# One of four normalisation tiles per attention head moved from GpSimd to VectorE, in a one-layer language-model tower on one core

## The reference, cut to what matters

```python
att = jnp.einsum('bhqd,bhkd->bhqk', q, k) / np.float32(np.sqrt(D))
att = att + jnp.exp(alibi_log_slopes)[None, :, None, None] * rel[None, None]
mask = pos[:, None] >= pos[None, :]
att = jnp.where(mask[None, None], att, -jnp.inf)
m = jnp.max(att, axis=-1, keepdims=True)
e = jnp.exp(att - m)
att = e / (1.0 + jnp.sum(e, axis=-1, keepdims=True))
out = jnp.einsum('bhqk,bhkd->bhqd', att, v)
```

## Time and profile before

| | us |
|---|---|
| median of 3 executions | 945.58 (944.63 to 945.79) |
| the profiled execution | 943.51 |
| its span | 941.7 |
| granted TensorE clock, mean of the span | 0.996 |

### The profile page before, as it was taken

The page is one execution under the profiler, slowest core; times in us unless marked ns, Lnnn a source line. Parts: engine busy times, 40 slices in busy tenths (PEclk is TensorE's granted clock), DMA queues, the critical chain, the costliest instruction groups (busy, mean ns, idle before and its releaser), DMA issues.

```text
span 941.7 us, 16997 instructions
## 1 busy us (share of the span) xinstructions
PE 872.0 (93%) x5660; PEld 680.4 (72%) x5660; DVE 581.7 (62%) x1779; ACT 728.0 (77%) x1622; POOL 627.7 (67%) x599
## 2 busy tenths in 40 slices
PE   7999978999999998999999999999899999999997
PEld 6888856777866786577766876777667866787585
DVE  5565636776684658475847575756756684658434
ACT  6855348998689869996889688877888689869843
POOL 6000069899686878688767878596868686868630
PEclk9999999999999999999999999999999999999999
DMA  9333360001000200020000100010001000000000
GB/s 262 73 112 112 125 190 1 1 1 56 2 1 1 79 1 2 1 73 7 2 1 24 56 1 1 23 58 1 1 23 57 1 1 1 23 2 1 1 23 23
DMA packets 23605, 33.56 MB, mean 36 GB/s; under 512 B 2608, under 2 KB 20176, under 8 KB 23520
## 3 DMA queue, kind: packets, MB, share of 16 engines
q1 hardware_dynamic: 19760, 19.01, 6.3%
q0 software_dynamic: 3760, 13.48, 5.0%
HBM read 17.80 MB, written 14.68 MB: 34 GB/s over the span
## 4 chain that ended last, share of the span: by engine, by line
PE 49%; ACT 13%; POOL 11%; issue 8%; DVE 6%; DMA 0%; POOLq 0%; DVEq 0%; ACTq 0%
PE ps L1388 12%; PE ps L1192 12%; POOL probs L783 9%; PE ps L1372 8%; PE ps L1360 5%; ACT probs L822 5%; PE ps L1361 4%; ACT turned_sb L829 4%; PE ps L1340 3%; DVE probs L994 2%; POOL token_rows L771 2%; PE ps L1200 1%; ACT k_hi L844 1%; ACT q_both L839 1%; PE ps L1334 1%
## 5 line engine op out<-in xcount | busy, mean ns | idle before, releaser
L783 POOL TENSOR_SCALAR probs<-probs,sums 128x512 f32<-128x512 f32 (+3 forms) x512 | 545.2, 1083 | 155.0 <-DVE sums L1001 154.6
L994 DVE CUSTOM_DVE_ANT_0 probs<-ps,causal,slope 128x512 f32<-128x512 f32 (+3 forms) x512 | 260.0, 547 | 162.0 <-PE ps L1361 161.5
L822 ACT ACTIVATE probs<-probs 128x513 f32<-128x513 f32 (+3 forms) x512 | 283.8, 556 | 34.9 <-DVE probs L994 27.4
L829 ACT ACTIVATE turned_sb<-ps 128x1280 f32<-128x1280 f32 x128 | 157.1, 1228 | 59.3 <-PE ps L1372 59.2
L1360 PE MATMUL ps<-k_hi,q_both 128*128 128x512 f32 (+3 forms) x512 | 181.0, 354 | 19.2 <-DVE probs L994 18.3
L1372 PE MATMUL ps<-ident,probs 128*128 128x128 f32 x1280 | 162.1, 274 | 5.3 <-POOL probs L783 5.3
L1388 PE MATMUL ps<-turned_sb,token_rows 128*64 128x512 f32 (+3 forms) x1024 | 152.0, 438 | 13.5 <-ACT turned_sb L829 13.5
L1361 PE MATMUL ps<-k_lo,q_both 128*128 128x512 f32 (+3 forms) x512 | 152.6, 324 | 0.0
L1372 PEld LDWEIGHTS ps<-ident,probs 128*128 128x128 f32 x1280 | 143.7, 142 | 6.8 <-POOL probs L783 6.5
L1388 PEld LDWEIGHTS ps<-turned_sb,token_rows 128*64 128x64 f32 x1024 | 75.2, 136 | 98.6 <-issue 82.6
L1360 PEld LDWEIGHTS ps<-k_hi,q_both 128*128 128x128 f32 x512 | 96.6, 189 | 61.1 <-DVE probs L994 34.9
(11 more groups left out here) (225 smaller groups left out, 1443.9 us busy)
## 6 DMA issues: line engine op xcount, KB each, us to landing
out_dram<-token_rows SPq DMA_DIRECT2D x7, 512.0 KB, 2.9
token_table<-made SPq DMA_DIRECT2D x4, 768.0 KB, 4.0
rows<-in_L_tok_codebook_dram SPq DMA_DIRECT2D x4, 512.0 KB, 9.9
w_f<-in_L_tok_W_dram SPq DMA_DIRECT2D x8, 256.0 KB, 6.1
early_rows<-made SPq DMA_DIRECT2D x4, 512.0 KB, 3.0
early_values<-xn SPq DMA_DIRECT2D x4, 512.0 KB, 3.0
token_table<-xn SPq DMA_DIRECT2D x4, 512.0 KB, 4.8
wo_f<-in_L_attn_Wo_dram POOLq DMA_DIRECT2D x1, 1024.0 KB, 10.3
```

Of the source, the lines that this page charges most:

```text
L783: ins = pool.tensor_scalar(at, at, recip[:, s % P_RING, q:q + 1], None, ALU.mult)
L822: act.activation(at, at, ACT.Exp, bias=least, scale=-1.0, accum_out=sums[:, s % P_RING, q:q + 1]).then_inc(exped, 1)
L829: act.activation(turned_sb[:, s % 2, :], turn_ps, ACT.Copy).then_inc(moved, 1)
L994: dve.tensor_tensor_reduce(out=probs[:, s % P_RING, start:end], in0=bank(unit % 2)[:, UNIT_AT[q]:UNIT_AT[q] + P * (q + 1)], in1=causal[:, ...
```

## The change

GpSimd no longer normalises row tile 0 of a head, the 128x128 block. VectorE does, in the next slot, behind the first minimum of the next head. TensorE's `turn` waits for both engines.

```diff
+    first_normed = sem("first_normed")
...
             def normalize(s):
                 pool.wait_ge(recip_done, s + 1)
-                for q in Q_ORDER:
+                for q in (3, 2, 1):
                     at = probs[:, s % P_RING, P_AT[q]:P_AT[q] + P * (q + 1)]
                     ins = pool.tensor_scalar(at, at, recip[:, s % P_RING, q:q + 1], None, ALU.mult)
                 ins.then_inc(normed, 1)
...
+            def normalize_first(s):
+
+                at = probs[:, s % P_RING, P_AT[0]:P_AT[0] + P]
+                dve.wait_ge(recip_done, s + 1)
+                dve.tensor_scalar(at, at, recip[:, s % P_RING, 0:1], None, ALU.mult).then_inc(first_normed, 1)
...
                 if s < ALL:
                     least_of(s, 0)
+                if 1 <= s <= ALL:
+                    normalize_first(s - 1)
+                if s < ALL:
                     least_of(s, 1)
                     least_of(s, 2)
...
             def turn(s):
                 pe.wait_ge(normed, s + 1)
+                pe.wait_ge(first_normed, s + 1)
```

## The result

The changed kernel takes **936.86 us** (median, 936.22 to 937.74) where the kernel before takes 945.68 on the same chip: ratio 0.9912, 95% interval 0.99 to 0.9925. It is 8.8 us faster. The forecast was 965.1 with 83% on slower, so the sign and the range are wrong. The profiled execution took 937.74 us, with a span of 935.9; TensorE's granted clock is 0.995 (0.996 before), so the clock plays no part.

The account below looks back on a forecast made before the run. TensorE was taken as the kernel's clock, GpSimd bounding only behind each gather. GpSimd's -5.3 us and VectorE's +3.1 and +21.7 made +19.5 us: 963.0 profiled, 965.1 as median; range from 947, its own upper end 984.

Parts of the forecast that it names:

- the two rows of 0.52 and 0.21 us: In the norm, VectorE's 128x4 tensor_scalar beside GpSimd's 128x128: both ended 0.03 us behind GpSimd's tile, read as a hold.
- The arrivals: VectorE reaches its new instruction at 187.69 and 412.97, inside GpSimd's 128x512; held 0.76 and 1.05 us to the tile's end.
- VectorE's terms: Cost of holds on VectorE's 128 new instructions reaching TensorE: +3.1 us in the first element, +21.7 in the seven later ones.
- 2.6 us per element in slots 7 to 12: Later elements: 1.5 us in slots 7 to 9 ahead of xn, 0.6 at slot 11 (y_lo), 0.5 at slot 12.
- The 0.5 us for slot 1: Later elements, slot 1 splitting K: the hold beyond VectorE's 0.56 us idle time delays k_lo and the turned copy, 0.5 us.
- The term for the opening slots: First element's two opening slots, where GpSimd still gathers: the new instruction costs 2 x 0.26 us.
- GpSimd's term: Behind the gathers, all six TensorE waits for GpSimd's normalisation go: -5.3 us, called the most this side can give.
- Rival 1: No hold worth the name, the tensor_scalar takes 0.26 us everywhere: -2.3 us, 943.3; chance 0.11.
- the new group's mean: Sign to check: VectorE's new x128 group averages near 1.0 us; 0.34 would be rival 1, 0.6 rival 2.
- Rival 2: Hold bounded at 0.35 us beyond the plain duration, instruction 0.6 us: +1.6 us, 947.2; chance 0.08.
- rival 3: GpSimd's next tile, 128x384, gets in first on some 60 uncovered slots: +75 us more, 1040; chance 0.04.
- Rival 4: VectorE's entries delay GpSimd's next tile, some 0.2 of 0.60 us per head returns: 1 us in all; no chance given.

Follow-up runs that it names:

- the probe: 105 trials behind the end of the kernel before: one GpSimd tensor_scalar of 512 to 128 columns against one delayed VectorE instruction; only the trace read, no kernel time.
- experiments 1, 4 and 6: 1: changed kernel without VectorE's normalisation of tile 0, ratio 0.9882; 4: changed kernel again, 0.9919; 6: VectorE's tile on heads 0, 1, 7, 8, 0.9887, and 1 again, 0.9879.
- experiment 2: Kernel before, GpSimd keeping all four tiles, plus an unused 128x128 tensor_scalar on VectorE at the same place: 945.74 us against 944.59, ratio 1.0005.
- the relief alone: Changed kernel with VectorE's new instruction and TensorE's wait left out, so row tile 0 is not normalised: 933.71 us, ratio 0.9882; repeated 933.51 us, 0.9879.
- the four-head version: Changed kernel with VectorE taking tile 0 only for heads 0, 1, 7 and 8 of each element: 934.45 us, ratio 0.9889; repeated 934.18 us, 0.9887.
- `early`: Changed kernel with VectorE's new instruction ahead of the first minimum, right behind the reciprocal that releases GpSimd: 938.25 us, ratio 0.9928.

## Why the prediction was wrong

**The step that failed is the reading of the earlier trace rows**: "VectorE's tensor_scalar is held until GpSimd's current instruction is over." The hold is no property of the whole tile. It comes in two stretches with a free one between, and the rows from which I read it were of 128 and 256 columns, where the probe has the instruction free at one or two of its starts 0.1 us apart, against four at 512 columns. Of the two rows of 0.52 and 0.21 us, the second was no hold: the probe's 128x4 lasts 0.22 us alone, so that it ended 0.03 us behind the tile was chance. xn's first 128x256, issued 0.52 us into a 128x256, was held by the second stretch, which I then carried over to the first half of a 128x512. The 0.52 us row itself is not reproduced: the probe's 128x4 issued 0.12 us into a lone 128x128 tile ends at 0.39, that of the trace at 0.62. That is 0.03 us behind the tile's end, where the probe's 128x4 ends from the second hold (0.02), so it looks as if it had missed the free stretch, as the one at 0.16 us above; GpSimd's tiles follow each other in both, and why they miss it stays open.

**The arrivals were right and decided the other way.** The earlier trace rows put VectorE at 0.80 and 0.51 us behind the start of GpSimd's 128x512. Both lie in the free stretch. In the changed kernel 28 of the new instructions start at about 0.5 us (0.45 to 0.55) and 22 at 0.8, with means of 288 and 283 ns. The timeline of both cases of the earlier trace rows after, and of one that meets a 128x384:

```profile
188.10 1.57 POOL L784 TENSOR_SCALAR probs<-probs,sums 128x512 f32<-128x512 f32 x1 [1.66 <-DVE sums L1002]
188.91 0.28 DVE L1008 TENSOR_SCALAR probs<-probs,sums 128x128 f32<-128x128 f32 x1
...
191.77 1.57 POOL L784 TENSOR_SCALAR probs<-probs,sums 128x512 f32<-128x512 f32 x1
192.18 0.36 DVE L1008 TENSOR_SCALAR probs<-probs,sums 128x128 f32<-128x128 f32 x1
...
337.30 1.25 POOL L784 TENSOR_SCALAR probs<-probs,sums 128x384 f32<-128x384 f32 x1
337.50 0.47 DVE L1008 TENSOR_SCALAR probs<-probs,sums 128x128 f32<-128x128 f32 x1
```

At 0.81 it is free. At 0.41 it ends 0.77 us into the tile, and at 0.20 into the 128x384 it ends 0.67 into it: the ends of the probe's first hold (0.763 and 0.656). The forecast had 0.76 to 1.05 us in nearly every slot; the kernel has 0.28 in 77 of 128. That the arrivals fell into the free stretch is luck of this order of work, and nothing in the forecast foresaw it.

**VectorE's terms** (+3.1 and +21.7 us) all hung on that hold. Measured, they are 3 to 4 us (experiments 1, 4 and 6) and under 1.4 in the kernel before (experiment 2). The turned copies show where: the 3.0 us lie between heads 6 and 10, whose copies are made in slots 9 to 13. The forecast had 2.6 us per element in slots 7 to 12, 18.2 in all, so it named the right place with six times the price. The 0.5 us for slot 1 did not come: heads 0 to 2 are as far ahead as with the relief alone. The term for the opening slots, 0.5 us, lies between the 1.0 and 0.35 us of two executions.

**GpSimd's term**, -5.3 us, was half of the 11 us that the relief alone gives, and for two reasons. (The turned copies place 10.1 of the 11; the rest is not placed.)
- I said "that is also the most that this side can give". But the earlier trace rows themselves showed GpSimd holding the norm of VectorE, and that norm ends in xn, for which TensorE waited 8.5 us. I had both rows and used them against the change only. The earlier GpSimd is through with its tiles, the quicker the norm is. The groups of the norm before, and then in the four-head version (repeated run):

```profile
L982 DVE TENSOR_SCALAR xn<-token_rows,mv,guess 128x256 f32<-128x256 f32 x28 | 10.6, 436 | 0.3
L977 DVE TENSOR_TENSOR guess<-guess,tmp 128x4 f32<-128x4 f32 x7 | 2.8, 405 | 0.2
L973 DVE TENSOR_TENSOR tmp<-tmp,var 128x4 f32<-128x4 f32 x7 | 1.8, 258 | 0.2
L975 DVE TENSOR_SCALAR tmp<-tmp 128x4 f32<-128x4 f32 x7 | 1.8, 258 | 0.2
```

```profile
L984 DVE TENSOR_SCALAR xn<-token_rows,mv,guess 128x256 f32<-128x256 f32 x28 | 9.7, 409 | 0.5 <-DVE guess L979 0.3
...
L977 DVE TENSOR_SCALAR tmp<-tmp 128x4 f32<-128x4 f32 x7 | 1.2, 170 | 0.2
L979 DVE TENSOR_TENSOR guess<-guess,tmp 128x4 f32<-128x4 f32 x7 | 1.1, 163 | 0.2
L975 DVE TENSOR_TENSOR tmp<-tmp,var 128x4 f32<-128x4 f32 x7 | 1.1, 162 | 0.2
```

The three small instructions take 0.43 us less per element (921 ns against 495) and the four xn 0.1 us less (27 ns each): 0.5 us per element, and xn's wait falls from 8.5 to 4.8 us in all. That is 3.7 us, as much as the turned copies show at the norms.
- The six waits for the turn are 5.3 us by TensorE's matmuls, but the clock of the turned copies gives 6.3. The row for its weight loads, which stand at the head of that chain, has 6.5 us. It is from the view of waits of the kernel before:

```profile
PEld ps L1372 <- POOL probs L783: 6.5, 6, 1.2
```

**The rivals.** Rival 1 had the instruction right in the mean (0.34 us named, 0.348 measured) and its sign, with a chance of 0.11; its 943.3 us is 6.4 too high, because it took the relief from the same -5.3. But it said "no hold", and there is one: the mean is made of 77 instructions at 0.28 us and 51 that took longer, so that its 0.34 fits is in part chance. Rival 2's 0.6 us and rival 3 are out by the same row. Rival 4, relief partly given back, did not show: GpSimd's 128x512 grew by 4 ns. What would show the forecast wrong was named: the new group's mean.

By the Trainium skill (SBUF — State Buffer, "Who interferes with whom") of a VectorE instruction in a two-port mode and one of GpSimd the one that comes first keeps the other out for the whole instruction. The sum that I made by that rule is 28 us off, and the probe does not bear it out: between 0.52 and 0.82 us of a 1.56 us tile VectorE is not kept out at all. The measurement decides.

## What to carry to other kernels

When two engines get in each other's way, find out at which moments of the instruction they do: one long instruction can have room for the other in its middle, and a row of a short one tells nothing of that. When an engine is relieved, count not only who waits for it but also whom it holds up while it works; in this kernel that was 3.8 of 10.1 us. And move only the work whose lateness costs something: four of sixteen heads gave all of the relief that can be measured, and VectorE's price fell from 3 or 4 us to 0.7.

## What the hardware showed that I had not expected

- A lone GpSimd tensor_scalar holds VectorE's in two stretches. VectorE's 128x128 ends 0.44, 0.55, 0.66 and 0.76 us into tiles of 128, 256, 384 and 512 columns, or 0.08 us behind the tile's end. Less the 0.28 us that it takes by itself, the stretches end at about 0.17, 0.27, 0.38 and 0.49 us, and 0.20 us ahead of the tile's end; this is an estimate. VectorE's 128x4, which takes 0.22 us, gives the same moments: it ends at 0.705 and 1.585 us into a 128x512, so it is let go at 0.49 and 1.37.
- A tensor_tensor of two SBUF inputs, 128x128, is held only in the first (issued 0.12 to 0.52 us into a 128x512 it ends at 0.828 each time); issued later, in 12 trials of 12, it takes 0.28 us, the whole second stretch included. So the two stretches could be GpSimd's reading and its writing, with the first meeting both of VectorE's forms and the second the tensor_scalar alone. That is inference; the trials show the times.
- In the trials whoever holds is not disturbed, and where VectorE is first GpSimd pays little. VectorE's instruction issued 0.02 us into a 128x512 takes 0.28 us and GpSimd's 1.65 instead of 1.56. Issued late in the free stretch it takes 0.28 us as well, and GpSimd's tile is 0.01 to 0.04 us longer (0.643 instead of 0.602 for 128 columns, issued at 0.22). `early` shows the same in the kernel (1634 ns against 1567), which is likely why its place costs only about 1 us.
